# Attention's filler products moved ahead of the next unit's rows

## The chip, the cores and the metric

The kernel runs on one core of a Trainium2 chip. The metric is the device time of one execution in microseconds (us), as a median over runs. Busy times, waits and starts are those of one profiled execution, counted from the start of its span.

## The reference, cut to what matters

The program is a small network on 2 x 1024 tokens of width 512: a gated recurrent layer, a feed-forward layer, differential attention, and the feed-forward layer again. Only attention is touched by the change:

```python
q1 = _split_heads(x @ Wq1, H);  q2 = _split_heads(x @ Wq2, H)
k = _split_heads(x @ Wk, H);    v = _split_heads(x @ Wv, H)
scores = jnp.einsum('bhqd,bhkd->bhqk', q, k2) * scale      # q of both sets, k2 = k twice
scores = jnp.where(causal, scores, jnp.finfo(scores.dtype).min)
p = jax.nn.softmax(scores, axis=-1)
y = jnp.einsum('bhqk,bhkd->bhqd', p, v2)
y = y1 - lam * y2
return y.transpose(0, 2, 1, 3).reshape(B, T, D) @ Wo
```

In the kernel's run T is 1024, with 16 heads of 32 channels.

## The kernel before

The attention phase works on 16 units, numbered 0 to 15. A unit is one turn `r` (a batch and four heads, 128 channels) with one of the two query sets: even units take the first set, odd units the second. A unit has 12 steps (`STEPS`), one for each block of 128 keys against a chunk of 512 queries: steps 0 to 3 are the first chunk, 4 to 11 the second. All work of TensorE stands in one order, written out by hand. In step i of unit u it issues

- `scores(u, i)`: products of keys with queries (L1078), the subtracted row maximum as a second product (L1084), and on diagonal blocks a mask (L1091). ScalarE then takes the exponential (L1210), in two halves.
- `weigh` of the step before: the probabilities times the values (L1114).
- the rows (`row`, L1061, with the mask L1067) of the next unit: the same scores with queries as output rows, from which VectorE takes the maxima (`row` on VectorE, L1290). Steps 0, 1 and 4 to 9 have one row block, steps 2 and 3 have two, steps 10 and 11 none. A row block is 128, 256, 384 or 512 columns wide; those at steps 3 (first), 5, 7 and 8 are 512 wide without a mask.
- the filler products (`fill`) that `slot_jobs` gives to the step: projections of the next turn's keys, queries and values (`k`, `q` L984, `v` L1014), the sum over the probabilities (`den` L1022), the output projection of a finished turn (`out` L1032), the transposed maxima (`neg` L1026), and in the last two units transposes for the next layer's normalisation (`norm` L1037).

Score pairs and row pairs share three pairs of PSUM banks in turn (`PAIR_USES`). `take_pair` waits for the use three places earlier: rows of a step wait for the first half of that step's exponential, and the scores of the next step wait for the first maximum of the row block just before them. A score or row function waits for both of its pairs before its first product:

```python
if kind == "row":
    pe.wait_ge(row_max, (u * NR + s) * 2 + a + 1)
else:
    pe.wait_ge(exped, (u * NS + s) * 2 + a + 1)
```

All filler products use bank 7. ScalarE copies most of them out, after the exponentials of the step. VectorE adds the `out` products to x (`finish`, L1346). VectorE also inverts the sums (`invert`, L1316, steps 2, 3, 6, 7), forms the output part (`take`, L1327, L1330, L1332, steps 4 and 8), and turns the maxima into three bf16 parts (`negate`, L1300 to L1306, step 10). GpSimd adds the probabilities up (`add_up`, L1259), and spreads the maxima (L1244).

Of the kernel before, what the change touches and what calls it, by code (L numbers as in the profile page):

```python
# [769 lines left out]
def step_width(s):  # L770
    c, kt = STEPS[s]
    return max(kt * P - c * BLK, 0)
# [13 lines left out]
def slot_jobs(u, i):  # L786

    r, w = divmod(u, 2)
    more, jobs = r + 1 < TURNS, []
    pair = r // 2 + 1  # L790
    if i == 1 and u:
        jobs.append(("den", u - 1, 1))
    if i == 5:
        jobs.append(("den", u, 0))
    if w == 0:
        if more:
            if i == 0:
                jobs.append(("k", r + 1, 0))
            if i == 2:
                jobs.append(("k", r + 1, 1))  # L800
            if i == 3:
                jobs.append(("q", r + 1, 0, 0))
            if i == 6:
                jobs.append(("q", r + 1, 0, 1))
        if r == 0 and i in (1, 4):
            jobs.append(("v", 0, 2 + i // 4))
        if r and i in (7, 8, 9, 11):
            jobs.append(("out", r - 1, {7: 4, 8: 5, 9: 6, 11: 7}[i]))
    else:
        if more and i in (0, 2):  # L810
            jobs.append(("q", r + 1, 1, i // 2))
        if pair < TURNS // 2 and i in (3, 6):
            jobs.append(("v", pair, 2 * (r % 2) + i // 6))
        if i in (9, 11):
            jobs += [("out", r, 0)] if i == 9 else [("out", r, 2), ("out", r, 3)]
        if i == 10:
            jobs.append(("out", r, 1))
    if i == 10 and u + 1 < UNITS:
        jobs.append(("neg", u + 1))
    if u in NORM_UNITS and i in NORM_SLOTS:  # L820
        jobs.append(("norm", NORM_UNITS.index(u), NORM_SLOTS.index(i)))
    return jobs


NORM_UNITS = [UNITS - 2, UNITS - 1]
NORM_SLOTS = [2, 3, 4, 6]
# [6 lines left out]
NTH = {job: n for n, job in enumerate(JOBS)}  # L833
assert len(NTH) == len(JOBS)
ON_DVE = [job[0] in ("out", "norm") for job in JOBS]
# [21 lines left out]
def phase_attention(nc, core, wq1, wq2, wk, wv, wlam, wo):  # L857
    with ExitStack() as ctx:
# [51 lines left out]
        def held(u, s):  # L910

            c, kt = STEPS[s]
            if kt == 0:
                return heads(total[(u * CQ + c) % 2])
            return heads(prob[(summed_by(u, s) - 1) % 2])
# [55 lines left out]
        def _(pe):  # L971
# [124 lines left out]
            def weigh(u, s):  # L1096
                c, kt = STEPS[s]
                r, w = divmod(u, 2)
                off = step_width(s)
                first, final = kt == 0, s == CHUNK_LAST[c]  # L1100
                if first and u * CQ + c:
                    pe.wait_ge(y_copied, u * CQ + c)
                if first and c == 0 and u == 0:
                    pe.wait_ge(fill_copied, FREED_BY_ACT[NTH[("q", 0, 1, 0)]])
                if first and c == 0 and w == 0 and r % 2 == 0:
                    pe.wait_ge(fill_copied, FREED_BY_ACT[NTH[("v", r // 2, 1)]])
                if first and c == 1 and w == 0 and r == 0:
                    pe.wait_ge(fill_copied, FREED_BY_ACT[NTH[("v", 0, 3)]])
                elif first and c == 0 and w == 0 and r % 2 == 0 and r:
                    pe.wait_ge(fill_copied, FREED_BY_ACT[NTH[("v", r // 2, 3)]])  # L1110
                for j in range(HPT):
                    pe.wait_ge(exped, (u * NS + s) * 2 + j // 2 + 1)
                    at = kt * 2 * P + r % 2 * P + (w * 2 + j % 2) * HD
                    last = pe.matmul(bank[6][HEAD_AT[j] * HD:(HEAD_AT[j] + 1) * HD, off:BLK],  # L1114
                                     v_rows[r // 2 % 2][:, at:at + HD], held(u, s)[:, j, off:BLK],
                                     start=first, stop=final)
                last.then_inc(weighed, 1)
# [11 lines left out]
            for u in range(UNITS):  # L1129
                n = 0  # L1130
                for i in range(NS):
                    scores(u, i)
                    if u * NS + i:
                        weigh(*divmod(u * NS + i - 1, NS))
                    if u + 1 < UNITS:
                        for _ in ROW_SLOTS[i]:
                            row(u + 1, n)
                            n += 1
                    for job in slot_jobs(u, i):
                        fill(job)  # L1140
            weigh(UNITS - 1, NS - 1)
            for job in EPILOGUE:
# [128 lines left out]
        def _(dve):  # L1271
# [22 lines left out]
            def negate(u):  # L1294
                dve.wait_ge(row_max, (u + 1) * 2 * NR)
                if u:
                    dve.wait_ge(filled, NTH[("neg", u - 1)] + 1)
                part_of = neg2[:, :].rearrange("p (h n q) -> p n h q", h=HPT, n=4)
                r_of = rounded[:, :].rearrange("p (h q) -> p h q", h=HPT)
                v.did(dve.tensor_reduce(part_of[:, 0], maxima[u % 2][:, :].rearrange(  # L1300
                    "p (h q c) -> p h q c", h=HPT, q=QT), AX.X, ALU.max, negate=True))
                v.settle()
                for n in range(2):
                    v.did(dve.tensor_copy(r_of, part_of[:, n]))
                    v.settle()
                    v.did(dve.tensor_tensor(part_of[:, n + 1], part_of[:, n], r_of, ALU.subtract))  # L1306
                    v.settle()
                dve.sem_inc(neg_ready, 1)
# [27 lines left out]
            def finish(job):  # L1336
                n, kind = NTH[job], job[0]
                src = bank[JOB_BANK[n]]
                if kind == "out":
                    _, r, t = job  # L1340
                    b, h = divmod(r, HT)
                    if h:
                        dve.wait_ge(fill_added, FREED_BY_DVE[NTH[("out", r - 1, t)]])
                    dve.wait_ge(filled, n + 1)
                    xt = x[:, (b * QT + t) * D:(b * QT + t + 1) * D]
                    dve.tensor_tensor(xt, xt, src, ALU.add).then_inc(fill_added, 1)  # L1346
                else:
                    _, blk, t = job
                    dve.wait_ge(high_kept, blk * TPB + t + 1)
                    dve.tensor_tensor(norm.half(blk, 1, t), src.rearrange("p (k t) -> p k t", k=KT),  # L1350
                                      norm.half(blk, 0, t), ALU.subtract).then_inc(fill_added, 1)
# [17 lines left out]
            def early_turn(blk, t):  # L1369
                n = blk * TPB + t  # L1370
                if n == 0:
                    dve.wait_ge(early_root, 1)
                    v.did(dve.reciprocal(e_inv[:, :], e_root[:, :]))
                    v.settle()
                if n >= 2:
                    dve.wait_ge(filled, NTH[("norm", *divmod(n - 2, TPB))] + 1)
                dve.tensor_scalar(early_rows[t % 2][:, :], x[:, n * D:(n + 1) * D], e_mv[:, 2 * n:2 * n + 1],
                                  e_inv[:, n:n + 1], ALU.subtract, ALU.mult).then_inc(turn_ready, 1)
# [4 lines left out]
            for u in range(UNITS):  # L1383
                n = 0
                for i in range(NS):
                    if i == NS - 2 and u + 1 < UNITS:
                        negate(u + 1)
                    if u + 1 < UNITS:
                        for _ in ROW_SLOTS[i]:
                            row(u + 1, n)  # L1390
                            n += 1
                    if i in (2, 3) and u:
                        invert(u - 1, 1, i - 2)
                    if i == 4 and u:
                        take(u - 1, 1)
                    if i in (6, 7):
                        invert(u, 0, i - 6)
                    if i == 8:
                        take(u, 0)
                    if u == NORM_UNITS[0] - 1 and 4 <= i < 4 + QT // 2:  # L1400
                        early_stats(i - 4)
                    if u in NORM_UNITS and i in NORM_SLOTS:
                        early_turn(NORM_UNITS.index(u), NORM_SLOTS.index(i))
                    for job in slot_jobs(u, i):
                        if ON_DVE[NTH[job]]:
                            finish(job)
            for half in range(2):
                invert(UNITS - 1, 1, half)
            take(UNITS - 1, 1)
# [80 lines left out]
```

## Time and profile before

| what | value |
|---|---|
| median of 3 runs | 2632.41 us (2631.1 to 2633.35) |
| the profiled execution, its own time | 2623.8 us |
| its span, first to last instruction | 2622.0 us |
| TensorE busy in the span | 2156.6 us (82%) |
| VectorE, ScalarE, GpSimd busy | 1448.8, 892.2, 817.3 us |
| attention's steps in the span | 1015 to 2225 us |

The profiled execution lies 8.6 us under the median. Its 1.8 us outside the span are start and end. Busy shares are averages over four layers; what a change in attention is worth has to be read from the 1210 us of its steps. In a timeline row the bracket at its end is the time that the engine sat idle before it, with what ended that time.

### The profile page before, as it was taken

The page shows a single profiled execution, that of the slowest core. Times are in us where ns is not written, and L with a number is a line of the kernel's source. Part 1 is how long each engine was busy: PE and PEld are TensorE (multiplying, and loading weights), DVE is VectorE, ACT ScalarE, POOL GpSimd, SP SyncE. Part 2 cuts the span into 40 slices and gives each one's busy share as a digit, 9 for nine tenths or more (in the row PEclk, how much of TensorE's full clock was granted, in tenths as well). Part 3 has the DMA queues.
Part 4 walks back from the last instruction along what each step waited for, and adds up shares of the span by engine and source line. Part 5 has one row for each costly group of instructions (what it writes and reads, how often), then busy time and mean ns, then how long its engine had stood idle before and what let it go on. Part 6 is the DMA issues. An engine that isn't in the chain of part 4 may idle for free. (4 is left out here: it accounts for less than half of the span.)

```text
span 2622.0 us, 32745 instructions
## 1 busy us (share of the span) xinstructions
PE 2156.6 (82%) x11664; PEld 918.0 (35%) x11664; DVE 1448.8 (55%) x1917; ACT 892.2 (34%) x1367; POOL 817.3 (31%) x395
## 2 busy tenths in 40 slices
PE   5888887789898878878788787888878766699998
PEld 2333333344444333332333333233333222344443
DVE  4878687836754523455545555544545645457544
ACT  2534343424433212333333233333333224144331
POOL 1656373600000001545434454543445436000000
PEclk8998999889999889999999999999999879799999
DMA  4100000020000020000000000000000000200000
GB/s 172 37 20 29 21 31 21 23 97 1 1 1 0 0 50 22 2 12 9 17 9 17 1 13 13 9 17 9 5 1 13 1 9 1 97 1 17 1 16 32
DMA packets 60766, 55.40 MB, mean 21 GB/s; under 512 B 36288, under 2 KB 44480, under 8 KB 60384
## 3 DMA queue, kind: packets, MB, share of 16 engines
q1 hardware_dynamic: 60640, 53.65, 6.4%
q8 instruction: 87, 1.43, 0.2%
q14 instruction: 39, 0.32, 0.0%
HBM read 43.02 MB, written 10.62 MB: 20 GB/s over the span
## 5 line engine op out<-in xcount | busy, mean ns | idle before, releaser
L1259 POOL TENSOR_TENSOR b_total<-b_total,b_prob 128x2048 f32<-128x2048 f32 (+3 forms) x160 | 518.1, 3238 | 652.6 <-ACT b_prob L1210 651.6
L1290 DVE TENSOR_REDUCE b_maxima<-psum 128x2 f32<-128x1024 f32 (+3 forms) x384 | 348.3, 953 | 530.8 <-PE psum L1067 355.4
L532 PE MATMUL psum<-hT,W 128*128 (+1 forms) x2048 | 451.9, 384 | 16.8 <-DMA W<-ternary 7.5
L1210 ACT ACTIVATE b_prob<-psum 128x1024 f32<-128x1024 f32 (+3 forms) x320 | 228.3, 766 | 300.5 <-PE psum L1091 214.0
L280 PE MATMUL psum<-hT,a_win 128*128 (+1 forms) x640 | 317.2, 647 | 5.8 <-DMA a_win<-in_w_inT 5.8
L532 PEld LDWEIGHTS psum<-hT,W 128*128 128x128 bf16 x2048 | 202.0, 99 | 265.7 <-issue 27.3
L1061 PE MATMUL psum<-b_kT,b_qT 32*128 32x512 f32 (+3 forms) x1536 | 184.4, 547 | 107.8 <-DVE b_maxima L1290 47.0
L1078 PE MATMUL psum<-b_qT,b_kT 32*128 32x512 f32 (+3 forms) x1536 | 195.2, 579 | 57.5 <-DVE b_maxima L1290 54.9
L667 DVE SCALAR_TENSOR_TENSOR f_h<-psum,f_sg 128x512 f32<-128x512 f32 x128 | 88.3, 691 | 223.5 <-ACT f_sg L592 221.8
L558 PE MATMUL psum<-W,f_hi 128*128 128x512 bf16 x512 | 196.3, 383 | 4.0 <-DVEq L653 3.2
L558 PE MATMUL psum<-W,f_lo 128*128 128x512 bf16 x512 | 196.2, 383 | 0.0
L280 PEld LDWEIGHTS psum<-hT,a_win 128*128 128x128 f32 x640 | 132.2, 210 | 164.8 <-issue 155.6
L592 ACT ACTIVATE f_sg<-psum 128x512 f32<-128x512 f32 x128 | 76.2, 597 | 283.6 <-PE psum L532 282.1
L1061 PEld LDWEIGHTS psum<-b_kT,b_qT 32*128 32x128 f32 x1536 | 67.1, 188 | 234.8 <-issue 226.0
L368 POOL TENSOR_TENSOR a_sign<-a_sign,a_hit 128x512 bf16<-128x512 bf16 x48 | 74.4, 1550 | 232.9 <-DVE a_hit L411 232.9
L1114 PE MATMUL psum<-b_prob,b_v_rows 128*32 128x512 f32 (+3 forms) x1280 | 136.8, 501 | 0.0
L1236 POOL MEMSET b_mask<- 128x128 f32 x1 | 0.2, 205 | 428.2 <-POOLq L485 428.2
L1078 PEld LDWEIGHTS psum<-b_qT,b_kT 32*128 32x128 f32 x1536 | 67.5, 199 | 187.9 <-issue 177.4
L984 PE MATMUL psum<-hT,b_wq 128*128 128x512 f32 x256 | 123.0, 625 | 0.6 <-ACT b_qT L1172 0.6
L1032 PE MATMUL psum<-b_wo,b_yT 128*128 128x512 f32 x128 | 86.5, 767 | 43.0 <-DVEq L1334 33.1
L1316 DVE RECIPROCAL b_rden<-b_rden 128x128 f32<-128x128 f32 x128 | 112.1, 918 | 11.6 <-ACT b_rden L1184 11.6
L682 DVE TENSOR_TENSOR f_lo<-f_h,f_hi 128x512 f16<-128x512 f32 x128 | 87.9, 686 | 39.8 <-ACT f_hi L607 39.2
(158 smaller groups left out, 2706.3 us busy)
## 6 DMA issues: line engine op xcount, KB each, us to landing
a_stage<-in_w_guT SPq DMA_DIRECT2D x32, 256.0 KB, 2.7
ternary<-W SPq DMA_DIRECT2D x1, 6144.0 KB, 17.9
a_win<-in_w_inT SPq DMA_DIRECT2D x5, 1024.0 KB, 9.0
x<-in_x SPq DMA_DIRECT2D x4, 1024.0 KB, 8.9
a_stage<-in_w_pT SPq DMA_DIRECT2D x16, 256.0 KB, 2.5
b_wq<-in_wq SPq DMA_DIRECT2D x64, 64.0 KB, 2.6
b_lamT<-lam_rows SPq DMA_DIRECT2D x32, 128.0 KB, 2.7
W<-ternary SPq DMA_DIRECT2D x8, 512.0 KB, 7.7
```

The lines of the kernel that those rows point to most:

```text
L280: last = pe.matmul(bank[n % 4][:, :], win[:, k * 5 * D + COL[name] + c * P:k * 5 * D + COL[name] + (c + 1) * P], core["hT"][:, ds(i * (KT ...
L532: last = pe.matmul(dst[:, :], W[:, k * 2 * HID + col:k * 2 * HID + col + P], hT[:, ds(i * (2 * KT * BLK) + (half * KT + k) * BLK, BLK)], s ...
L558: last = pe.matmul(bank[4 + t][:, :], src[:, m * BLK + t * P:m * BLK + (t + 1) * P], W[:, KT * 2 * HID + m * D:KT * 2 * HID + (m + 1) * D] ...
L667: dve.scalar_tensor_tensor(h[:, m * BLK:(m + 1) * BLK], bank[m % 2 * 2 + 1][:, :], 1.0 / UP, sg[m % 2][:, :], ALU.mult, ALU.mult).then_inc ...
L984: last = pe.matmul(to, weights[:, k * P:(k + 1) * P], hT[:, (blk * KT + k) * BLK:(blk * KT + k + 1) * BLK], start=(k == 0), stop=(k == KT ...
L1061: last = pe.matmul(to[j // 2][:, j % 2, 0:width], strip(qT[w][r % 2], j, qt * P, (qt + 1) * P), strip(kT[w][r % 2], j, kc * BLK, hi), star ...
L1078: pe.matmul(to[j // 2][:, j % 2, off:BLK], strip(kT[w][r % 2], j, kt * P, (kt + 1) * P), strip(qT[w][r % 2], j, c * BLK + off, (c + 1) * B ...
L1114: last = pe.matmul(bank[6][HEAD_AT[j] * HD:(HEAD_AT[j] + 1) * HD, off:BLK], v_rows[r // 2 % 2][:, at:at + HD], held(u, s)[:, j, off:BLK], ...
L1210: act.activation(held(u, s)[:, 2 * a:2 * a + 2, off:BLK], pair_banks(("score", u, s, a))[:, :, off:BLK], ACT.Exp, scale=SCALE).then_inc(ex ...
L1259: pool.tensor_tensor(acc, acc, held(u, s)[:, :, off:BLK], ALU.add).then_inc(summed, 1)
L1290: dve.tensor_reduce(maxima[u % 2][:, :].rearrange("p (h q c) -> p h q c", h=HPT, q=QT)[:, 2 * a:2 * a + 2, qt, kc], pair_banks(("row", u, ...
L1316: v.did(dve.reciprocal(rden[k % 2][:, cols], rden[k % 2][:, cols]))
```

## The change

On TensorE the filler products of a step are issued between `weigh` and the rows, except `neg`, which stays behind. On VectorE, the sums with x (and the early rows and halves of the normalisation) are issued before the row maxima, inversions and `take` of the same step. No instruction is added or removed, and the bank rotation is as it was.

```diff
@@ attention, TensorE
                     scores(u, i)
                     if u * NS + i:
                         weigh(*divmod(u * NS + i - 1, NS))
+                    late = [job for job in slot_jobs(u, i) if job[0] == "neg"]
+                    for job in slot_jobs(u, i):
+                        if job not in late:
+                            fill(job)
                     if u + 1 < UNITS:
                         for _ in ROW_SLOTS[i]:
                             row(u + 1, n)
                             n += 1
-                    for job in slot_jobs(u, i):
+                    for job in late:
                         fill(job)
@@ attention, VectorE
                     if i == NS - 2 and u + 1 < UNITS:
                         negate(u + 1)
+                    if u in NORM_UNITS and i in NORM_SLOTS:
+                        early_turn(NORM_UNITS.index(u), NORM_SLOTS.index(i))
+                    for job in slot_jobs(u, i):
+                        if ON_DVE[NTH[job]]:
+                            finish(job)
                     if u + 1 < UNITS:
                         for _ in ROW_SLOTS[i]:
                             row(u + 1, n)
...
                     if u == NORM_UNITS[0] - 1 and 4 <= i < 4 + QT // 2:
                         early_stats(i - 4)
-                    if u in NORM_UNITS and i in NORM_SLOTS:
-                        early_turn(NORM_UNITS.index(u), NORM_SLOTS.index(i))
-                    for job in slot_jobs(u, i):
-                        if ON_DVE[NTH[job]]:
-                            finish(job)
```

TensorE, step 3 of an even unit (two row blocks, and the projection of the next turn's queries, L984), as a piece of the difference:

```order
+L984 MATMUL psum<-hT,b_wq 128x512 x4
 L1061 MATMUL psum<-b_kT,b_qT 128x512 x4
 L1061 MATMUL psum<-b_kT,b_qT 128x256 x4
 L1067 MATMUL psum<-b_ident_b,b_later_key 128x128 x4
-L984 MATMUL psum<-hT,b_wq 128x512 x4
 L1078 MATMUL psum<-b_qT,b_kT 128x512 x4
 L1084 MATMUL psum<-b_bias,b_ones_b 128x512 x4
```

The projection has moved from between the second row block and step 4's scores (L1078) to ahead of the first row block. Nothing stands any longer between the last row block and the scores.

TensorE, step 9 of an odd unit, where the first output product of the turn (L1032) stands:

```order
 L1091 MATMUL psum<-b_later_key,b_ident_b 128x128 x4
 L1114 MATMUL psum<-b_prob,b_v_rows 32x512 x4
-L1061 MATMUL psum<-b_kT,b_qT 128x512 x4
-L1067 MATMUL psum<-b_ident_b,b_later_key 128x128 x4
-L1032 MATMUL psum<-b_wo,b_yT 128x512
+L1032 MATMUL psum<-b_wo,b_yT 128x512
+L1061 MATMUL psum<-b_kT,b_qT 128x512 x4
+L1067 MATMUL psum<-b_ident_b,b_later_key 128x128 x4
 L1078 MATMUL psum<-b_qT,b_kT 128x256 x4
 L1084 MATMUL psum<-b_bias,b_ones_b 128x256 x4
```

The last row block of the next unit now stands behind the output product, and with it behind that product's wait for `take`.

VectorE, steps 7 to 9 of an even unit up to `negate`, before:

```order
L1290 TENSOR_REDUCE b_maxima<-psum 128x2 x2
L1316 RECIPROCAL b_rden<-b_rden 128x128 x2
L1346 TENSOR_TENSOR x<-x,psum 128x512
L1290 TENSOR_REDUCE b_maxima<-psum 128x2 x2
L1327 TENSOR_TENSOR b_yT<-b_y_part,b_rden 128x512
L1346 TENSOR_TENSOR x<-x,psum 128x512
L1290 TENSOR_REDUCE b_maxima<-psum 128x2 x2
L1346 TENSOR_TENSOR x<-x,psum 128x512
L1300 TENSOR_REDUCE b_neg<-b_maxima 128x4x8
```

The same with the change (its line numbers are four higher):

```order
L1350 TENSOR_TENSOR x<-x,psum 128x512
L1294 TENSOR_REDUCE b_maxima<-psum 128x2 x2
L1320 RECIPROCAL b_rden<-b_rden 128x128 x2
L1350 TENSOR_TENSOR x<-x,psum 128x512
L1294 TENSOR_REDUCE b_maxima<-psum 128x2 x2
L1331 TENSOR_TENSOR b_yT<-b_y_part,b_rden 128x512
L1350 TENSOR_TENSOR x<-x,psum 128x512
L1294 TENSOR_REDUCE b_maxima<-psum 128x2 x2
L1304 TENSOR_REDUCE b_neg<-b_maxima 128x4x8
```

Each sum with x has moved ahead of the maxima of its step, and `negate` follows the last maxima directly.

## Rows read from the trace of the kernel before

**Rows 1.** Waits from 1015 to 2225 us: waiter, releaser, total, times, longest

```profile
PE psum L1078 <- DVE b_maxima L1290: 54.9, 63, 5.8
PE psum L1061 <- ACT b_prob L1210: 34.2, 73, 1.6
PE psum L1061 <- ACT b_total L1210: 25.8, 30, 1.5
PE psum L1037 <- DVE b_early_rows L1377: 23.8, 8, 4.7
```

**Rows 2.** Windows: length, busy us of each engine, granted clock, DMA

```profile
1401.00:1478.00 77.00, 61.39 (x485) 25.88 (x477) 39.45 (x45) 22.98 (x33) 34.40 (x12) 0.96 0.07 15
1478.00:1555.00 77.00, 63.24 (x457) 23.44 (x455) 38.25 (x45) 26.52 (x39) 34.38 (x12) 0.93 0.03 8
2094.00:2178.00 84.00, 57.88 (x453) 21.21 (x445) 43.47 (x54) 25.76 (x36) 34.39 (x12) 0.82 0.02 7
```

**Rows 3.** Timeline of TensorE, steps 6 to 10 of odd unit 5

```profile
1440.22 1.06 PE L1114 MATMUL psum<-b_prob,b_v_rows 128*32 128x512 f32 x8
1441.57 0.93 PE L1061 MATMUL psum<-b_kT,b_qT 32*128 32x384 f32 x8 [0.28 <-ACT b_prob L1210]
...
1442.66 3.67 PE L1014 MATMUL psum<-b_wv,hT 128*128 128x256 f32 x16
1446.26 1.14 PE L1078 MATMUL psum<-b_qT,b_kT 32*128 32x512 f32 x8
...
1459.22 1.14 PE L1061 MATMUL psum<-b_kT,b_qT 32*128 32x512 f32 x8
...
1464.97 2.04 PE L1032 MATMUL psum<-b_wo,b_yT 128*128 128x512 f32 x2 [4.28 <-DVEq L1334]
1466.94 1.24 PE L1078 MATMUL psum<-b_qT,b_kT 32*128 32x256 f32 x8
...
1471.81 0.33 PE L1026 MATMUL psum<-ident,b_neg 128*128 128x128 f32 x1 [0.85 <-DVE x L1346]
```

**Rows 4.** Timeline of TensorE, scores behind rows with no filler (units 13, 14)

```profile
2040.59 1.14 PE L1078 MATMUL psum<-b_qT,b_kT 32*128 32x512 f32 x8 [0.77 <-DVE b_maxima L1290]
...
2055.57 1.14 PE L1078 MATMUL psum<-b_qT,b_kT 32*128 32x512 f32 x8 [1.03 <-DVE b_maxima L1290]
...
2097.07 1.45 PE L1078 MATMUL psum<-b_qT,b_kT 32*128 32x384 f32 x8 [0.50 <-DVE b_maxima L1290]
```

**Rows 5.** Timeline of TensorE, steps 1 and 3 of even unit 6

```profile
1487.06 0.71 PE L1061 MATMUL psum<-b_kT,b_qT 32*128 32x256 f32 x8 [1.07 <-ACT b_prob L1210]
...
1501.01 1.14 PE L1061 MATMUL psum<-b_kT,b_qT 32*128 32x512 f32 x8 [1.60 <-ACT b_prob L1210]
...
1505.12 4.51 PE L984 MATMUL psum<-hT,b_wq 128*128 128x512 f32 x8
```

**Rows 6.** Timeline of TensorE, step 8 of unit 6 to the next unit

```profile
1532.10 1.14 PE L1078 MATMUL psum<-b_qT,b_kT 32*128 32x512 f32 x8 [0.34 <-DVE b_maxima L1290]
...
1547.98 0.45 PE L1026 MATMUL psum<-ident,b_neg 128*128 128x128 f32 x1 [2.98 <-DVEq L1308]
...
1554.63 0.39 PE L1084 MATMUL psum<-b_bias,b_ones_b 32*128 32x512 bf16 x4
```

**Rows 7.** Timeline of VectorE, the last instruction of `negate` in unit 6

```profile
1545.47 2.31 DVE L1306 TENSOR_TENSOR b_neg<-b_neg,b_rounded 128x32 f32<-128x32 f32 x1
```

**Rows 8.** Timeline of TensorE, steps 8 to 10 of unit 0

```profile
1077.03 1.14 PE L1078 MATMUL psum<-b_qT,b_kT 32*128 32x512 f32 x8 [1.40 <-DVE b_maxima L1290]
...
1090.00 0.30 PE L1026 MATMUL psum<-ident,b_neg 128*128 128x128 f32 x1 [0.49 <-DVEq L1308]
```

**Rows 9.** Timeline of VectorE, the last instruction of `negate` in unit 0

```profile
1089.61 0.19 DVE L1306 TENSOR_TENSOR b_neg<-b_neg,b_rounded 128x32 f32<-128x32 f32 x1
```

**Rows 10.** Timeline of GpSimd, the addition at step 10 of units 0 and 6

```profile
1089.90 2.36 POOL L1259 TENSOR_TENSOR b_total<-b_total,b_prob 128x1024 f32<-128x1024 f32 x1 [0.81 <-ACT b_prob L1210]
...
1545.39 2.34 POOL L1259 TENSOR_TENSOR b_total<-b_total,b_prob 128x1024 f32<-128x1024 f32 x1 [1.23 <-ACT b_prob L1210]
```

## The prediction

> **What bounds the kernel now.** I read the waits of attention's stretch first. TensorE, issuing in one order, waits there for two partners. The next scores wait 54.9 us in 63 places for VectorE's row maxima; the rows wait 34.2 and 25.8 us for ScalarE's exponentials [rows 1]. So each step is a chain: scores, exponential, rows, maximum, next scores. A filler hides the link behind which it stands. Before, it stands between rows and scores and hides the maximum; the exponential has only `weigh` as cover. Afterwards it stands ahead of the rows and hides the exponential, and the maximum is bare.
>
> The timeline gives both prices. At step 6 of unit 5 the rows wait 0.28 for the exponential and the scores behind the filler wait for nothing; filler start to scores is 3.60 [rows 3]. Where no filler stands, the scores wait 0.50 behind rows 128 wide, 0.77 behind a pair 512 and 256 wide, 1.03 behind 384 [rows 4], and 1.40 behind 512 without a mask [rows 8]. With a filler of one product (0.34 at step 8 of unit 6 [rows 6]) part of the 1.40 is left already.
>
> The windows then show the granted clock: 0.96 over an odd unit, 0.93 over an even one, 0.82 over unit 14 [rows 2]. The clock falls to 1.2 GHz behind the long waits: the output product behind the 4.28 wait takes 2.04 [rows 3], and the projection behind the 1.60 wait takes 4.51 instead of 3.6 [rows 5]. So ends of units count twice, by the wait and by what runs slowly behind it.
>
> **Steps 0 to 6 and 7, price by price.** Each moved filler adds the bare maximum and takes off the exponential's wait and what was left of the maximum's. The idle column counts from a masked row's modelled end, a little after a filler could start, so I allow 0.15 more for each masked step (chosen; 0 to 0.2).
>
> An odd unit: step 0, 0.50 + 0.15 - 0.86 (25.8 / 30 [rows 1]) = -0.2. Step 1 is 256 wide, which no row shows bare: between 0.50 and 1.03 I take 0.77, the row whose last block is also 256; +0.9, with no exponential wait to remove. Steps 2 and 3, two row blocks each, +0.9 each; the wait of the second block for the first's maximum stays. Step 5, 1.40 - 0.28 - 0.34 = +0.8. Step 6, 1.03 + 0.15 - 0.28 = +0.9. Sum +4.2.
>
> An even unit differs in two steps, where the rows wait longer because ScalarE is still copying the key projection out: 1.07 at step 1 and 1.60 at step 3 [rows 5]. With the projection ahead of the rows these copies run under them. Step 1 becomes 0.9 - 1.07 = -0.2, step 3 0.9 - 1.60 = -0.7. Step 7 has an output product, +0.8. Steps 0 to 7: -0.2 - 0.2 + 0.9 - 0.7 + 0.8 + 0.9 + 0.8 = +2.3. The half clock behind the 1.60 should go as well: 0.9 on the projection and, estimated, 0.6 on the row block before it, so -1.5 (bound 0).
>
> **Step 9 of an odd unit.** The output product waits for `take` until 1464.97; the row block from 1459.22 on lay wholly inside that wait [rows 3]. `take` hangs on work ahead of step 9, which does not move, so the product still starts then. The row block now follows at 1466.94, at half clock (its products' 1.14 become about 2.0), plus 0.3 of mask and 1.4 of bare maximum: step 10's scores at about 1470.7 instead of 1466.94, +3.8. Step 10's own work, slow before (1.24 for scores 256 wide), is then at full clock, -1.0. So `neg`, which nothing else holds, slips by +2.8 from 1471.81. Bounds: 1.1 + 0.3 + 1.3 = 2.7, and 3.8 if the clock is not back in step 10. An odd unit: 4.2 + 2.8 = +7.0.
>
> **Steps 8 to 10 of an even unit.** Here `neg` waits 2.98 [rows 6], for the last instruction of `negate`, which takes 2.31 [rows 7] where the same instruction takes 0.19 in unit 0 [rows 9]. In unit 6 it begins 0.08 after GpSimd's addition and ends with it; in unit 0 it begins 0.29 before [rows 7, 9, 10]. VectorE is late there because the maxima queue behind the sum of step 8 and `take`, and `negate` behind the sum of step 9. The change puts both sums ahead, under waits for TensorE. Unit 0, which has no output products, already is what comes out: scores, bare maximum, rows, bare maximum, `neg` 12.97 after step 8's scores, its wait 0.49 [rows 8]. Two output products (2.04 at half clock, so about 1.05 each) and 0.2 less wait for the exponential give 14.9, against 15.88 in unit 6 [rows 6]: -1.0. Behind the 2.98 wait the clock is halved: 6.65 from `neg` to the next unit's L1084 [rows 6]. At full clock I estimate 3.65, somewhat over half: -3.0 (bound 0). An even unit: 2.3 - 1.5 - 1.0 - 3.0 = -3.2.
>
> The Trainium skill, page "SBUF — State Buffer", section "Who interferes with whom", says that a VectorE instruction with two SBUF inputs and a GpSimd instruction that reads SBUF exclude each other, and that the one which starts first holds the port. The trace agrees with its 2.31 against 0.19; by that rule a start 0.29 ahead is enough, as in the sum above, and a start behind is rival C.
>
> **The last units.** TensorE waits 23.8 us in eight places for the early rows of the normalisation, because VectorE makes them behind maxima and inversions [rows 1]. Now they come first. About 10 should remain (the inversions of the step before and GpSimd's additions still hold VectorE), and about 4 come back as bare maxima and as maxima that wait for the halves: -10. Unit 14's clock of 0.82 against 0.93 is 84 x 0.11 = 9 us of clock [rows 2]; I give back 7. Together -17 (bounds -8 and -29). At the very end GpSimd's additions bound unit 15, so its gain is small and inside this. Unit 13 has fillers at steps 0, 1, 2, 5 (+2.4) and a held `negate` like an even unit (-1.0 - 3.0): -1.6. Unit 0: even, without the output products: -0.6.
>
> **Sum.** Six odd units (1 to 11) +42, six even ones (2 to 12) -19, unit 0 -0.6, unit 13 -1.6, units 14 and 15 -17: +4. Against the profiled 2623.8 that is 2628; the change carries over to the median, 2632.4 + 4 = 2636. ScalarE and GpSimd get more room in every step, and the DMA queue's waits move by less than a step, so nothing is added for them. If ScalarE's key copies were not done before the next exponential, 1.07 and 1.60 would come back in part.
>
> **Rivals.**
>
> A, the sum above, 0.42: losses and gains nearly cancel, 2636, its own range 2626 to 2645.
>
> B, the clock does not come back, 0.28. For it speaks that bare maxima put more short waits into every step, against it that unit 13 already has steps without fillers, whose scores run at full speed (1.14 for 512 wide at 2040.59 and 2055.57 [rows 4]). If even units keep their slow stretches, 6 x 4.5 = 27 comes on top: 2663. If only step 3 is slow, in both kinds of unit, 1.5 x 6 kept and 1.5 x 6 new, 18 on top: 2654.
>
> The Trainium skill, page "TensorE: Matmul & The Clock Gate", Part 1, says that the throttled clock is the default and activity releases it. The half clock behind 4.28 agrees [rows 3]; a rule of activity alone speaks for B, since the change spreads idle time.
>
> C, GpSimd holds `negate` after all, 0.08. The margin is 0.29 [rows 9, 10]. Past it, `neg` comes 0.2 after the addition's end, 2.5 later than in A, and the half clock stays: 5.5 x 6 = 33, and in odd units, where a sum stands behind `negate`, some 1.3 x 6 = 8: 2677. It decides where `negate` starts 0.3 later relative to step 10's scores.
>
> D, the early rows cost nothing any longer, 0.22: all of the 23.8 goes, less 4 of bare maxima, and all 9 us of clock: -29 instead of -17, so 2624. For it: VectorE is idle over half of the time there (43.47 busy of 84 [rows 2]). Against: inversions of the step before still stand ahead of them.
>
> That the order changes nothing can be left out: 0.28 against 1.40 are prices of two different waits.
>
> **How the numbers follow.** About 0.2% (5.3 us) is what a measurement can tell from no change. D lies mostly below it (0.18 faster, 0.04 same). A: 0.06 faster, 0.27 same, 0.09 slower. B: 0.03 same, 0.25 slower. C slower. So 0.24, 0.34, 0.42. The range takes in D with a full even-unit gain (2617) and B (2662), and leaves out C and the tails, 2 in 10.
>
> **What would show it.** Scores waiting for maxima up from 54.9 to about 150 us, rows waiting for exponentials down to about 20; an even unit of about 73 us and an odd one of about 84 (each about 77 now); `neg` in even units behind a wait of 0.5 and full clock after it; the early rows' 23.8 down to about 10; row blocks of step 9 in odd units at half clock. The forecast is wrong if even units stay at 0.93 clock or if the last instruction of `negate` still takes over 2 us.

## The result, and the profile after

The changed kernel takes 2661.51 us (median of 4 runs, 2660.8 to 2662.51), the kernel before beside it 2632.88 (4 runs, 2631.1 to 2633.5): ratio 1.011, 95% interval 1.0093 to 1.0128. It is slower by 28.6 us. The sum of the prediction was +4, and its own range for that sum ended at 2645; the time lies inside the whole range only because that one takes in rival B (2654 to 2663). A second set of four runs of the same kernel has its median at 2668.95, 35.4 over the kernel before beside it (e9 below), which is above B's figures. The profiled execution of after took 2661.88 us, its span is 2660.1.

The waits of the changed kernel from 1015 to 2265 us (waiter, releaser, total, times, longest), which answer to [rows 1]:

```profile
PE psum L1078 <- DVE b_maxima L1294: 158.2, 150, 5.8
...
PE psum L1032 <- DVEq L1338: 40.4, 7, 6.1
PE psum L1061 <- ACT b_total L1214: 10.6, 14, 0.9
...
PE psum L1037 <- DVE b_early_rows L1381: 5.7, 4, 2.3
PE psum L1061 <- ACT b_prob L1214: 4.4, 18, 0.4
```

The exchange is there as foreseen: 54.9 of bare maxima became 158, the exponentials' 60 became 15, the early rows' 23.8 became 5.7. (L1338 is in `take`; the output products waited 26.6 us for it before, in as many places.) Three windows, with the columns of [rows 2], show what was not foreseen. The second is odd unit 5 and the third even unit 6; the first is even unit 4 with the last 9 us of unit 3 ahead of it:

```profile
1331.00:1415.00 84.00, 67.79 (x520) 25.59 (x520) 40.07 (x55) 28.43 (x44) 37.45 (x15) 0.98 0.03 7
1415.00:1500.00 85.00, 63.41 (x469) 27.04 (x465) 39.10 (x45) 22.87 (x33) 36.52 (x14) 0.92 0.06 13
1500.00:1576.00 76.00, 62.00 (x473) 23.21 (x472) 36.41 (x46) 26.41 (x39) 32.60 (x11) 0.98 0.03 8
```

The even unit has its clock (0.98; 0.93 in [rows 2]), the odd one has lost some (0.92; 0.96 in [rows 2]), and TensorE is busy for 63.4 us in it where it was for 61.4. The end of even unit 4, TensorE's timeline, answers to [rows 6]:

```profile
1409.29 0.71 PE L1078 MATMUL psum<-b_qT,b_kT 32*128 32x256 f32 x8 [1.30 <-DVE b_maxima L1294]
...
1411.62 0.30 PE L1026 MATMUL psum<-ident,b_neg 128*128 128x128 f32 x1 [0.39 <-DVEq L1312]
...
1415.25 0.39 PE L1084 MATMUL psum<-b_bias,b_ones_b 32*128 32x512 bf16 x4
```

`neg` waits 0.39, and from it to L1084 it is 3.63 us (6.65 in [rows 6]). The last instruction of `negate` on VectorE and the addition on GpSimd that held it before:

```profile
1411.22 0.19 DVE L1310 TENSOR_TENSOR b_neg<-b_neg,b_rounded 128x32 f32<-128x32 f32 x1
...
1411.61 2.35 POOL L1263 TENSOR_TENSOR b_total<-b_total,b_prob 128x1024 f32<-128x1024 f32 x1 [2.06 <-ACT b_prob L1214]
```

It takes 0.19 and starts 0.39 ahead of the addition [rows 7, 10: 2.31, behind it by 0.08]. Now odd unit 5, TensorE's timeline at steps 2 to 4 and 9 to 10, which answers to the end of [rows 3]:

```profile
1431.73 1.14 PE L1061 MATMUL psum<-b_kT,b_qT 32*128 32x512 f32 x8
...
1434.50 0.50 PE L1061 MATMUL psum<-b_kT,b_qT 32*128 32x128 f32 x8 [1.30 <-DVE b_maxima L1294]
...
1435.96 0.81 PE L1078 MATMUL psum<-b_qT,b_kT 32*128 32x128 f32 x8 [0.63 <-DVE b_maxima L1294]
...
1437.35 1.08 PE L1114 MATMUL psum<-b_prob,b_v_rows 128*32 128x256 f32 x8
...
1438.36 4.19 PE L1014 MATMUL psum<-b_wv,hT 128*128 128x256 f32 x16
...
1445.03 0.71 PE L1061 MATMUL psum<-b_kT,b_qT 32*128 32x256 f32 x8 [1.41 <-DVE b_maxima L1294]
...
1446.84 1.14 PE L1078 MATMUL psum<-b_qT,b_kT 32*128 32x512 f32 x8 [0.77 <-DVE b_maxima L1294]
...
1484.34 2.04 PE L1032 MATMUL psum<-b_wo,b_yT 128*128 128x512 f32 x2 [5.71 <-DVEq L1338]
1486.32 2.09 PE L1061 MATMUL psum<-b_kT,b_qT 32*128 32x512 f32 x8
...
1490.14 1.24 PE L1078 MATMUL psum<-b_qT,b_kT 32*128 32x256 f32 x8 [1.20 <-DVE b_maxima L1294]
```

Behind two short waits, 1.30 and 0.63, the scores 128 wide take 0.81, `weigh` 1.08 and the projection 4.19. At full clock the same program takes 0.50, 0.64 and 3.72 there (below, e9). Step 10 begins slow, too: its scores take 1.24, not 0.71.

**The step table.** From the timelines I took the time from each step's scores to the next step's in the changed kernel, and subtracted that of the kernel before (its second profiled execution, e0 below). A positive number is time lost by the change. Columns: steps 0 to 11, and the sum of the unit.

```
unit   0     1     2     3     4     5     6     7     8     9    10    11 |  sum
 5  -1.07  0.67  0.80  2.44  0.00  0.51  0.90  0.00  0.01  3.80  0.69  0.00 |  8.75
 6  -0.16 -0.44  0.80 -2.23  1.11  0.52  0.90  0.71  0.82  0.60 -2.73 -1.97 | -2.07
 9  -1.04  0.66  0.80  2.48  2.00  3.50  0.90 -0.01  0.01  3.80 -1.01  0.00 | 12.09
14  -0.95 -0.90 -2.32 -2.95 -3.91  1.00 -3.80 -0.97  0.81  0.59 -2.58 -0.60 |-16.58
```

Where the clock is whole (at 2.4 GHz all through), steps repeat to 0.02 us between units and executions; what differs, differs by 1 to 3.5 us at once, mostly at steps 3 to 5, 8 and 10. Units 1, 3, 7 and 11 give 10.37, 8.60, 8.86, 10.45; units 2, 4, 8, 10, 12 give -2.31, -2.02, -2.11, -0.15, 0.42; unit 0 -0.3, unit 13 -3.0, unit 15 -1.6.

**The clock's share.** A unit's length times one minus its granted clock says how many us of full clock it went without, idle time included, so it is a measure of the clock and not yet a price. Summed over units, in us, for the profiled execution of every run, with the median of its times (unit 0, left out here, has 3.1 in e0, 1.5 in after and 6.4 in e9):

```
run                        us       ratio  [95%]            odd 1-11  even 2-12  13-15
e0 before, again           2631.83                            26.3      24.4     35.0
after                      2661.51  1.0110 [1.0093 1.0128]    51.6      14.4     15.7
e9 after, again            2668.95  1.0125 [1.0106 1.0144]    50.9      18.2     25.2
e3 even units only         2602.73  0.9897 [0.9857 0.9937]    21.7      20.0     12.4
e4 odd units only          2686.37  1.0202 [1.0169 1.0236]    52.3      19.9     34.4
e1 TensorE's order alone   2714.56  1.0334 [1.0279 1.0389]    47.7      22.4     40.6
e5 step 9 back             2656.39  1.0102 [1.0073 1.0132]    51.5      22.1     26.0
e6 step 2 back             2649.07  1.0078 [1.0042 1.0114]    44.7      22.4     15.7
e11 steps 2, 3 back        2623.97  0.9971 [0.9959 0.9982]    21.1      12.2     20.8
e7 one sum behind negate   2596.25  0.9872 [0.9842 0.9903]    25.5       5.8     30.7
e8 chosen steps            2583.32  0.9824 [0.9792 0.9855]    24.1       5.8     22.4
e10 e8, output later       2598.63  0.9864 [0.9847 0.9880]    30.6       6.5     27.6
```

Ratios are to the kernel before run beside each. Its medians are 2632.88 beside after, 2634.13 beside e0 to e4, 2628.72 beside e5 to e8 and 2633.58 beside e9 to e11, so a difference of runs from two of these groups is better taken from each one's own kernel before.

### The profile page after: what moved, and what is told of

Read it like the earlier page. It is cut to its first block and busy times, and to the rows that moved or that the text cites. A ratio compares the mean times of both kernels' runs of the same rounds, so it can differ in the third digit from the quotient of the medians.

```text
span 2660.1 us, 32745 instructions
## 1 busy us (share of the span) xinstructions
PE 2162.7 (81%) x11664; PEld 924.1 (35%) x11664; DVE 1434.9 (54%) x1917; ACT 890.3 (33%) x1367; POOL 814.7 (31%) x395
## 5 line engine op out<-in xcount | busy, mean ns | idle before, releaser
L1078 PE MATMUL psum<-b_qT,b_kT 32*128 32x512 f32 (+3 forms) x1536 | 194.6, 575 | 161.8 <-DVE b_maxima L1294 158.2
L1078 PEld LDWEIGHTS psum<-b_qT,b_kT 32*128 32x128 f32 x1536 | 68.7, 196 | 234.2 <-issue 198.5
L1032 PE MATMUL psum<-b_wo,b_yT 128*128 128x512 f32 x128 | 80.6, 719 | 53.6 <-DVEq L1338 46.9
L984 PE MATMUL psum<-hT,b_wq 128*128 128x512 f32 x256 | 120.5, 615 | 0.6 <-ACT b_qT L1176 0.6
```

What stands on the lines that cost most here:

```text
L984: last = pe.matmul(to, weights[:, k * P:(k + 1) * P], hT[:, (blk * KT + k) * BLK:(blk * KT + k + 1) * BLK], start=(k == 0), stop=(k == KT ...
L1078: pe.matmul(to[j // 2][:, j % 2, off:BLK], strip(kT[w][r % 2], j, kt * P, (kt + 1) * P), strip(qT[w][r % 2], j, c * BLK + off, (c + 1) * B ...
```

## The experiments

In all edits a predicate `early(u, i, job)` replaces the change's test for `neg`, and VectorE makes a sum ahead of the rows where it is true, at its old place otherwise. In e1, e8 and e10 VectorE makes no sum ahead of the rows. The normalisation's pieces go by a switch of their own: early on both engines in all edits but e1, e4 and e7. The code below is cut to the line that differs.

```diff
-late = [job for job in slot_jobs(u, i) if job[0] == "neg"]
+late = [job for job in slot_jobs(u, i) if not early(u, i, job)]
```

**e0, the kernel before again.** No edit.

> The kernel before once more, for a profile that is compared with the change's step by step. Theory A (my terms are right in size, and what is missing is TensorE's clock at 1.2 GHz on steps 3 to 5 and 10): the time is near the median of 2633, while the profiled execution shown first was 2623.8, so this profile should show some more work at half clock than that one, in the normalisation of units 14 and 15 or outside attention; units 2 to 12 take 76.2 and 77.4 us again. Theory B (the two profiles differ by chance everywhere): the units themselves are longer by 0.5 us each.

Units 0 to 13 repeat to 0.02 us per step, and so does unit 14 up to its last step (0.6 apart), as theory A had it; the slow places of this kernel are the same in both executions. Unit 15 took 6.8 us longer than in the first profiled execution, and the span, 2630.0, now suits the median: the first execution (2623.8) was a short one. VectorE's timeline of e0 in unit 15:

```profile
2209.84 4.93 DVE L1330 TENSOR_TENSOR b_y_part<-b_y_part,b_lamT 128x512 f32<-128x512 f32 x1
...
2214.81 4.87 DVE L1332 TENSOR_TENSOR b_yT<-b_yT,b_y_part 128x512 f32<-128x512 f32 x1
```

In the first execution L1330 took 0.69 and only L1332 4.91. There it began at 2207.62 and GpSimd's next addition at 2208.14; in e0 that addition began at 2209.70, ahead of it. So instructions of `take`, too, can be caught by GpSimd's additions or get in before one, which is worth some 5 us at the end.

**e1, TensorE's order alone.** VectorE keeps its old order, and the normalisation's pieces stay where they were on both engines.

```diff
+    return job[0] != "neg"              # early, TensorE
+    return False                        # sum_first, VectorE
```

> TensorE's order is the change's, VectorE's stays as before (sums with x behind the maxima); the normalisation's pieces stay where they were on both. Theory A: in even units the maxima of step 9 come behind the sum of step 8, so negate starts about 0.7 us later against GpSimd's addition, its last instruction takes 2.3 us again and neg waits about 3 us with half clock behind it: some 5.6 us for each even unit; in odd units the sum of step 9 delays negate past the same edge, 2 to 3 us each; and units 14 and 15 lose what the early rows gave (11 us). Together 2661 + 34 + 15 + 11 = about 2720. Theory C (VectorE's order matters to no one): 2661 + 11 = 2672.

2714.56 us. The waits of e1 from 1015 us to the end of attention:

```profile
PE psum L1097 <- DVE b_maxima L1313: 153.1, 146, 5.2
...
PE psum L1045 <- DVEq L1331: 21.3, 8, 3.0
```

The maxima are as bare as in the changed kernel, and `neg` is still held, eight times for up to 3.0. Against the changed kernel e1 is some 52 us slower. By the step table 30 of them are in even units, where `negate` is held again because only VectorE's new order brings it ahead of the addition, 11 in unit 13 and 20 in unit 14, where the early rows come late again (21.8 us of waits for them, 5.7 in the changed kernel). The odd units are 6 shorter than in the changed kernel.

**e3 and e4, even or odd units only.** e3 moves the fillers and sums of even units and the normalisation's rows, e4 those of odd units.

```diff
+    return job[0] != "neg" and u % 2 == 0    # e3; e4: u % 2 == 1, normalisation as before
```

> Only even units and the normalisation's pieces (units 14 and 15) have the change's order, on both engines. Theory A: each even unit gains 1.4 us and the odd unit behind it 0.9 us at its step 0 (its clock is whole again behind neg); units 14 and 15 gain 11 us: 2633 - 8 - 6 - 11 = 2608. Theory D (moving fillers costs in every unit, because a bare maximum outweighs a bare exponential wherever it is done): 2633 + 10 = 2643.

> Only odd units have the change's order, on both engines, without the normalisation's pieces. Theory A: each odd unit 1 to 11 loses 9.6 us (bare maxima 3.6, step 3 at half clock 1.5, step 9 3.8, step 10 0.7) and unit 13 about 3: 2633 + 58 + 3 = 2694. If the half clock at step 3 of odd units comes only from what even units do ahead of them, 9 us less: 2685. Theory D: half of the change's loss, 2647.

e3 takes 2602.73, 31 less than the 2634.13 beside it; e4 takes 2686.37, 52 more. Together that is +21, to the whole change's +29. So the even units' and the normalisation's gain is real, and the odd units lose more than the 42 forecast. That e4 meets its 2685 is not for the reason given there: step 3 of units 1, 3 and 9 is at +2.48, +4.05 and +4.03, and the even units came out 5.8 shorter. The full clock they went without is 52.3 us in e4 and 21.7 in e3, where their fillers stay: the loss is made in the odd units alone.

**e5 and e6, one step of odd units back.**

```diff
+    return job[0] != "neg" and not (u % 2 == 1 and i == 9)   # e5; e6: i == 2
```

> The change, but in odd units the output product of step 9 and its sum stand where they stood before, so that the row block lies under the wait for take again. Theory A: step 9 gives back 3.8 us and step 10 about 0.7 in each of units 1 to 11, unit 13 gives 0.9: 2661 - 27 - 1 = 2633. The 1.2 GHz on steps 3 to 5 stays, since it comes from the waits around it. Theory E (the half clock of an odd unit comes from the end of the unit before or its own step 9): steps 3 to 5 are whole again too, another 20 us: 2613.

> The change, but in odd units the filler of step 2 stands behind the rows again. The bare wait between step 2's rows and step 3's scores (0.63) goes and 3.6 us of projection stand between the waits of step 2 and those of step 3. Theory A (the half clock at steps 3 to 5 is set off by bare waits standing close together there): besides 0.8 for the wait, the half clock there goes, 1.5 or more in each of six units: 2661 - 5 - 9 to 20 = 2627 to 2647. Theory F (step 3 is slow for another reason, such as ScalarE or VectorE being late): only the 0.8, 2656.

e5 gave the 3.8 back at step 9 in all six odd units, yet the kernel is 27.7 us over the one before beside it, where the change is 28.6 over its own: half clock turned up elsewhere (step 5 of units 3, 8, 9 and 11 at +3.51, +2.38, +2.53, +2.54, where the whole clock leaves +0.52). TensorE's timeline of e5, step 9 of unit 5: the row block is again inside the wait.

```profile
1481.91 2.04 PE L1051 MATMUL psum<-b_wo,b_yT 128*128 128x512 f32 x2 [4.28 <-DVEq L1357]
1483.89 1.24 PE L1097 MATMUL psum<-b_qT,b_kT 32*128 32x256 f32 x8
```

e6 set step 3 of all six odd units to +0.95, the price forecast for it at full clock (+0.9), where after had 0.95 to 4.03. But slow stretches came at steps 4, 5 and 8 instead (unit 3 +1.37, +2.76 and +1.34), and its six runs spread from 2640.74 to 2667.59. The kernel before spread less beside it (2623.08 to 2637.12 in nine runs). Neither expectation held fully: taking the wait away makes step 3 whole, but mostly moves the slow stretch (the steps at half clock) to a later step.

**e7, one sum behind `negate`.** The kernel before, in which VectorE makes the output sum of step 9 behind `negate`, in all units, not ahead of it (shortened; at its old place the sum is left out).

```diff
+                    if i == NS - 2:
+                        for job in slot_jobs(u, i - 1):
+                            if job[0] == "out":
+                                finish(job)          # behind negate(u + 1)
```

> The kernel before, in which VectorE alone has one edit: the sum of step 9 stands behind negate. Nothing is moved on TensorE. Theory A (negate is held only because it starts 0.1 us behind GpSimd's addition): its last instruction takes 0.19 again, neg waits about 0.5 instead of 2.98, the clock stays whole: 2.7 at step 10, 2.0 at step 11 and 1.0 at the next step 0 in each even unit, about as much in units 13 and 14: 2633 - 40 = 2593. Theory G (the two sums, not negate's start, were late; a waiting sum now holds bank 7 longer): neg only moves by 0.6, 2629.

2596.25, 2593 expected. VectorE's timeline of e7 in unit 6, and GpSimd's:

```profile
1536.01 0.19 DVE L1329 TENSOR_TENSOR b_neg<-b_neg,b_rounded 128x32 f32<-128x32 f32 x1
1536.42 0.69 DVE L1369 TENSOR_TENSOR x<-x,psum 128x512 f32<-128x512 f32 x1 [0.23 <-DVE b_neg L1329]
```

```profile
1536.40 2.35 POOL L1282 TENSOR_TENSOR b_total<-b_total,b_prob 128x1024 f32<-128x1024 f32 x1 [1.23 <-ACT b_prob L1233]
```

`negate` ends 0.2 before the addition begins. The place of one short sum gives 32 us against the 2628.72 beside it: in each even unit -2.0 at step 10, -2.0 at step 11, -0.9 in the next step 0. The even units go without 5.8 us of full clock where it was 24.4. These three places give 4.9 us, and the whole change gives 5.6 there; e7 has them without one new bare maximum.

**e9, the changed kernel again.** No edit.

> The changed kernel once more. Theory A (the places at half clock behind bare waits depend on where the clock's changes happen to fall, not on the unit): the profile's step lengths agree with the first one to 0.1 us wherever the clock was whole, while the extra 1.5 to 5 us at steps 3 to 5 sit in other units or at other steps; the runs spread over some 10 us around 2661, as those of the kernel with step 2 put back did (2641 to 2668). Theory H (they are fixed by the program): the same extras in the same units, spread under 3 us.

Its four runs lie from 2660.41 to 2675.67, where the first four lay within 1.7 us; the profiled one is the longest. TensorE's timeline of e9, the place in unit 5 that was slow above:

```profile
1446.21 0.50 PE L1078 MATMUL psum<-b_qT,b_kT 32*128 32x128 f32 x8 [0.63 <-DVE b_maxima L1294]
...
1447.03 0.64 PE L1114 MATMUL psum<-b_prob,b_v_rows 128*32 128x256 f32 x8
1447.60 3.72 PE L1014 MATMUL psum<-b_wv,hT 128*128 128x256 f32 x16
```

The same waits, the same 0.63, and the full clock: step 3 of units 5 and 7 is at +0.96 and +0.95, that of unit 9 at +4.08, and unit 3 has +2.01 and +3.51 at steps 4 and 5 where it had +0.01 and +0.52. Which place is slow is not fixed by the program. The sum over the odd units came out alike in these two executions (50.9 and 51.6 us), but the sum over all units did not (101 and 83 with unit 0), and the times of the two are 13.8 us apart.

**e11, steps 2 and 3 back in all units.**

```diff
+    return job[0] != "neg" and i not in (2, 3)      # the normalisation's stay early
```

> The change, but the fillers of steps 2 and 3 stand behind the rows again in all units, so that no bare maximum of the change's making is left between step 2's rows and step 4's scores. Theory A: step 2 gives 0.8 back in 13 units and step 3 of odd units 0.9, even units lose the 0.7 and 1.5 that the key copies had brought, and the half clock at steps 3 to 5 (1.5 to 5 us in 10 of 13 units) goes: 2661 - 10 - 5 + 13 - 27 = 2632. Theory F (steps 3 to 5 are slow for another reason): 2661 - 2 = 2659.

2623.97, ten runs of 2620.93 to 2631.81, less than theory A's 2632. In odd units steps 2, 3 and 4 stand within 0.02 of the kernel before, and the full clock gone without falls from 51.6 to 21.1 us. Against the span of after (2660.1 to 2623.0), 37 us came back. The steps' own prices are some 13 of it (0.8 at step 2 in fourteen units, 0.95 at step 3 in six, less the 0.7 that step 3 gained in six); the other 24, by subtraction, are clock. Not all of the half clock is gone: step 5 of units 1, 4, 6, 8 and 12 stands at +2.01 to +2.13, where the whole clock leaves +0.52, so in these units it moved to a later step, as in e5 and e6 (in unit 4 the scores at 1363.05 take 2.09, not 1.14, behind waits of 0.90 and 1.03). TensorE's timeline of e11 in unit 5, with the projection behind the waits of 1.30 and 1.40:

```profile
1418.33 0.50 PE L1080 MATMUL psum<-b_kT,b_qT 32*128 32x128 f32 x8 [1.30 <-DVE b_maxima L1313]
...
1418.99 3.65 PE L1003 MATMUL psum<-hT,b_wq 128*128 128x512 f32 x8
1422.58 0.50 PE L1097 MATMUL psum<-b_qT,b_kT 32*128 32x128 f32 x8
...
1426.54 0.71 PE L1080 MATMUL psum<-b_kT,b_qT 32*128 32x256 f32 x8 [1.40 <-DVE b_maxima L1313]
...
1427.42 3.67 PE L1033 MATMUL psum<-b_wv,hT 128*128 128x256 f32 x16
```

The 1.30 and 1.40 between two row blocks are those of the kernel before; with 3.6 us of filler between rows and scores no second wait follows them at once, and nothing slows in this unit.

**e8, chosen steps.** Moved early are only the fillers that gained by it (steps 0, 1 and 3 of even units) and the normalisation's rows; the sum of step 9 stands behind `negate`, as in e7.

```diff
+    return job[0] != "neg" and u % 2 == 0 and i in (0, 1, 3)
```

> Only the moves that paid in the change's trace, and negate ahead of step 9's sum: fillers ahead of the rows in steps 0, 1 and 3 of even units, the normalisation's pieces first in units 14 and 15, everything else as before. Theory A: e7's 40, and 0.15 + 0.45 + 2.24 = 2.8 for each even unit (17), and 16 for unit 14: 2633 - 40 - 17 - 14 = 2562. If the half clock comes back one step later, as at step 4 of even units in the change, 7 us more: 2569.

2583.32, the fastest version: 1.8% under before, though some 14 to 21 short of the expectation. Step 3 of even units gave 1.1 where 2.24 was counted on, and patches of half clock (1.2 at step 4 of units 6, 8 and 10, 1.3 at step 8 of units 5, 7, 9 and 11) took some back. Its waits for maxima, and those for exponentials:

```profile
PE psum L1097 <- DVE b_maxima L1313: 73.4, 89, 5.8
...
PE psum L1080 <- ACT b_total L1233: 17.7, 22, 0.9
PE psum L1080 <- ACT b_prob L1233: 14.2, 53, 0.5
```

**e10, e8 with the first two output products of odd units one step later,** to empty the 4.28 wait for `take`.

```diff
-        if i in (9, 11):
-            jobs += [("out", r, 0)] if i == 9 else [("out", r, 2), ("out", r, 3)]
+        if i == 11:
+            jobs += [("out", r, 1), ("out", r, 2), ("out", r, 3)]
         if i == 10:
-            jobs.append(("out", r, 1))
+            jobs.append(("out", r, 0))
```

> The version of e8, and in odd units the first output product goes from step 9 to step 10 and the second to step 11, so that TensorE has no product at step 9 that waits for take. Theory A: the 4.28 wait becomes a bare maximum of 1.3 and a rest of about 0.9 before the product; the third product at step 11 waits another 0.85 for its bank; with the half clock behind the long wait gone, 3 us for each odd unit: 2583 - 20 = 2563. Theory I (take, held by GpSimd, only moves the wait to step 10, at half clock as before): 2583 + 3.

2598.63, 15 more than e8 (10 when each is taken against its own kernel before), and more than either theory had. Step 9 gained 0.65 only, and steps 10 and 11 lost 0.5 and 1.97 (unit 1 lost 5.8 at step 11). The output products' wait for `take` did go, from 30.6 us in e8 to 1.2, but the waits for maxima rose from 73.4 to 108.8: the wait for `take` had covered work, and the product pushed to step 11 stands bare.

## Why the prediction was right and wrong, point by point

**The exchange of waits was right.** A step's direct price is what it costs with the clock whole. All of them held within 0.3, as the step table shows: step 0 -0.16 (-0.2 forecast), step 1 +0.67 in odd units (+0.9) and -0.45 in even ones (-0.2), step 2 +0.80 (+0.9), step 5 +0.52 (+0.8), step 6 +0.90 (+0.9), step 7 of even units +0.71 (+0.8), step 3 of odd units at full clock +0.95 (+0.9: e6, e9). Of the two choices that no row showed, the 0.77 for rows 256 wide is what that wait measures (0.77, step 2's scores of unit 5), and the 0.15 for a masked step was high.

**Step 9 of odd units: right.** +3.80 to +3.83, +3.8 forecast; the row block lay inside the wait for `take`, runs behind it at half clock (2.09), and its maximum is bare (1.20). e5 takes the same 3.8 off again. The prediction had the product start as before; it does (8.12 us behind step 9's scores, 8.14 before), and it is the row block's leaving this wait that lets TensorE's waits for `take` grow from 26.6 to 40.4 us.

**`negate` and the end of even units: right.** 0.19, 0.39 ahead of the addition; steps 8 to 10 without `neg`'s tail 0.82 + 0.60 - 2.73 = -1.3 (-1.0), from `neg` on -1.97 and -0.9 (-3.0). e1 (held again) and e7 (free again) show that the start decides it. The Trainium skill, page "SBUF — State Buffer", section "Who interferes with whom", says that whichever of the two starts first holds the port; that agrees with e7 (0.19 where it was 2.31) and with `take` in e0 (4.93 where it was 0.69). Rival C did not come.

**The normalisation: right in size.** Units 14 and 15 gave -18.1 (-17). The rows' wait fell further than forecast, to 5.7 (10), and the step table's gain is still only 18. Rival D's -29 did not come.

**The clock failed, and it is more than the whole miss.** The step of the prediction that failed is rival A's premise, that "losses and gains nearly cancel" with the half clock gone from step 3 and from step 10: two terms were mis-sized and one was missing. Together they came out some 36 us worse than forecast, while the direct prices and the last units came out about 10 better.

First, the -1.5 of even units, given because "the half clock behind the 1.60 should go as well". Step 3 did fall by 2.23, where the wait's part of it was 0.7. But +1.1 came at step 4 of units 2 to 8 instead and +1.7 in unit 12, which had 1.9 more at step 5, too; in unit 10 step 3 stayed at +0.73. That is 11 us. With the books kept as in the prediction (what the even unit's end gives at the next step 0 belongs to the even unit) the six even units gave -13.7, not -19.

Second, the -1.0 at step 10 of odd units came in units 3, 9 and 11 only; in units 5 and 7 it is +0.7, and in unit 1 +0.1. The output product waits 5.71 where it waited 4.28, and after that the clock is not always back by step 10. This was the bound 3.8 named.

Third, the missing term was a new half clock in odd units at steps 3 to 5: 1.5 in units 1, 5, 7 and 9, 3.1 in unit 3, and 2.0 and 3.0 at steps 4 and 5 in units 9 and 11. It sums to 4 x 1.5 + 3.1 + 2 x 5.0 + 1.1 (unit 1, step 4) = 20 us. The odd units gave +64 in the same books, where +42 was forecast: these 20, 4.5 at step 10, less 3 by which the direct prices were high. With -13.7, unit 0's -0.3, unit 13's -2.1 and the last two units' -18, the sum is +30, which is the difference of the two spans (2660.1 and 2630.0); 28.6 was measured between the medians.

Rival B said "bare maxima put more short waits into every step" and gave 2654 to 2663; in kind it was what happened, with 0.28 on it. Its nearest form is the second, a slow step 3 in both kinds of unit at 18 us; 31 came at steps 3 to 5. Its first form did not come: the slow ends of even units went. What spoke against it, the scores of unit 13 at 1.14 behind 0.77 and 1.03 [rows 4], was a weak reason: they tell of those places alone. Where odd units turned slow, steps 2 and 3 have two row blocks each, whose own wait for the first's maximum (1.30, 1.41) was there before; the change set a second bare wait (0.63, 0.77) right behind each, where a filler of 3.6 us had stood. e11 shows that the new half clock hangs on these fillers: with those of steps 2 and 3 back, 30 us of the missing full clock in odd units are gone; e3 and e4 show that it hangs on the odd units' own. That it is the nearness of two waits, and not the idle time of the whole stretch, is argued and not shown: e11 takes away both and still has slow scores at step 5 of even units, behind waits 2.3 us apart, and e6, which takes away one wait, only moves the slow stretch. Open, too, is what fixes the place in one execution: the two profiles of the changed kernel (after and e9) have it in different places, and no run here controls it. Of the Trainium skill, the page "TensorE: Matmul & The Clock Gate", Part 1, has activity release the clock; e11, which spreads the same work with fewer short waits (51.6 to 21.1 us), agrees.

**The signs named in advance:** maxima 158 (about 150) right, exponentials 15 (about 20) right, `neg` 0.39 (0.5) right; the early rows' 5.7 (about 10) better than said. From one unit's first scores to the next unit's, where the prediction comes to 74 for an even unit and 83.4 for an odd one (its 73 and 84, with the 0.9 at step 0 counted in the odd unit), the even ones take 74.2 to 74.3 in units 2 to 8, 76.1 in unit 10 and 76.7 in unit 12: right in four of six. The odd ones take 86.0 to 89.3: wrong, and that is where the forecast failed. The two signs that were to refute it, even units at 0.93 clock and a `negate` over 2 us, did not come (unit 12 alone is at 0.93); no sign watched the odd units' clock, 0.87 to 0.92.

## What to carry to other kernels

Price the clock of a moved wait by its neighbours: a bare wait (one with no other work behind which to hide) of 0.5 to 1.4 us mostly cost itself, but where it followed another with no filler between them, steps here took 1.5 to 5 us more at 1.2 GHz, and removing just one wait moved the slow stretch on. Split a change that gains in one kind of stage and loses in another (even and odd units here) before accepting or dropping it: the halves were -31 and +52 us, the chosen pieces -45. Look for instructions whose duration jumps (0.19 to 2.31 us) and move what stands ahead of them first; that one edit beat the whole change by 61 us, each taken against its own kernel before.

## What the runs showed of the hardware that was not expected

The place of the half clock can differ between executions of one program: in unit 3 of the changed kernel step 3 is at +4.03 in one profile and +2.47 in the other, with +2.01 and +3.51 more at the next two steps. e9's four runs span 15 us and e6's six 27 us. It is not so in every program: the kernel before has its slow steps at the same places, to 0.02 us, in both profiles up to unit 13. Work at full clock repeats to 0.02 us per step in all of them.

Whether VectorE gets in ahead of a GpSimd addition can be chance as well: the same instruction of `take` in unit 15 took 0.69 in one execution and 4.93 us in another, and unit 15 was 6.8 us longer in the second.
